# Delta-rule stage: key and query products on each head's own 64 rows instead of zero-padded keys, and output products that alternate between two heads

## The chip, the core and the metric

The kernel runs on one core of a Trainium2 chip. The metric is the device time of one execution in microseconds. It is a whole decoder of four layers in one launch; the change touches the first of its fifteen stages, the attention of layer 0, which fills roughly the first 3.9 ms.

## What is computed

The stage computes a gated delta rule for a batch of B = 16 sequences of T = 128 tokens and D = 256 channels, with 8 heads of 64 channels and M = 8 modes a head. Each mode rotates keys and queries by its own angles and has its own decay and step size:

```python
H, DK, DV, M = (8, 64, 64, 8)
q = (x @ Wq).reshape(B, T, H, DK)     # k, v alike
beta = sigmoid((x @ Wbeta).reshape(B, T, H, M))
tg = sigmoid((x @ Wtg).reshape(B, T, H, M))
qr = _l2norm(_rotary(q, cos, sin)) * scale
kr = _l2norm(_rotary(k, cos, sin))
g = log(clip(tg * rho, 1e-06))
def step(S, inp):                      # one token, for all modes, sequences and heads
    S = S * exp(b_g)
    kv = einsum('mbhk,mbhkv->mbhv', k_t, S)
    dv = (v_t - kv) * b_beta
    S = S + k_t[..., :, None] * dv[..., None, :]
    o_t = einsum('mbhk,mbhkv->mbhv', q_t, S)
o = einsum('tmbhv,hm->bthv', ys, softmax(mode_logits)) * sigmoid(x @ Wg)
x = layernorm(x + o @ Wo)
```

## The kernel before

The 16 sequences are 16 turns of one loop, each engine running its own instruction stream and meeting the others at semaphores. A turn does not step through tokens. For each of the 64 chains (8 heads x 8 modes) it forms two 128 x 128 matrices, key against key and key against query, multiplies them by the decays between tokens, inverts the lower triangular system in 32 x 32 blocks, and multiplies the solution by the key-query matrix. All of it is float32; one float32 `nc.tensor.matmul` shows in the trace as two MATMUL records, each with an LDWEIGHTS record.

A turn has two halves (`hf`) of 4 heads each. A half has 8 groups `i` of 4 chains, and 4 packs `p` of two groups. A pair of heads shares one 128-row tile: head 0 of the pair has its 64 channels on rows 0 to 63, head 1 on rows 64 to 127. Group `i` holds 4 modes of one head.

**Products.** For each pack, VectorE multiplies the keys and queries of a pair of heads by cosines (L951) and sines (L954), 4 modes at a time, GpSimd adds the two (L689) into `kq`, and ScalarE copies the keys of each head into `kz` (L880): `kz` holds zeros in the rows of the other head, written once (L658). For each group GpSimd spreads the decays under a mask (L684), TensorE sums them up to exponents (L764, and L765 in bfloat16, banks 0 and 1), ScalarE takes the exponential into `Bt` (L884), and TensorE multiplies the padded keys by keys and queries: 4 matmuls of 128 x 128 weights and 256 columns (L773) into two banks. VectorE then makes the coupling matrix `Lt` from them (L971, 4 a group) and the output matrix in place in `Bt` (L979). The products of group `i` wait until L979 is through with group `i - 2`, which used the same banks.

**Inverse.** `invert` on VectorE: transposes of the diagonal blocks (L1004), then a serial chain of 60 small operations (L1013, L1014). The products of the second half are worked off between the links of the first half's inverse: VectorE runs L951, L954, L971 and L979 of half 1 there, in a list (`between`) written out by hand.

**Solution.** TensorE solves 4 block rows `q` of 32 tokens: L793 and L796 couple a row to those before it, L806 applies the inverse. Their tiles are 32 to 128 rows by 32 columns, with 64 moving columns. ScalarE (L895, L899) or VectorE (L1024) evacuate them. Ahead of each group of 16 records a small bfloat16 matmul, `carrier` (L714), takes the wait. When a head's last block row is solved, GpSimd weights it (L696, `weighted`).

**Output.** L818: for each head 8 matmuls (modes) of 128 x 64 weights and 128 columns accumulate in bank 2, for an even head in partitions 0 to 63, for an odd one in 64 to 127. VectorE gates the result (L1030), L823 projects it after the second half, L128 to L154 add and normalise it, and the next turn starts at L745. The order on TensorE in a turn is: L745 to L750, products of both halves, L720 and L725 for the next turn, solution of half 0, output of half 0, solution of half 1, output of half 1, L823.

## Time and profile before

| | us |
|---|---|
| median of 3 runs | 8310.44 |
| lowest and highest of them | 8294.9, 8350.9 |
| span of the profiled execution | 8333.2 |

The profiled execution is 23 us (0.3%) over the median, and inside the runs' own spread. Over the whole span TensorE is busy 81%, VectorE 48%, ScalarE 22%, GpSimd 17%. The delta-rule turns fill 97 to 3925 us; there TensorE is busy 3292 us, VectorE 2048 us, ScalarE 860 us and GpSimd 867 us of 3828, at a mean granted TensorE clock of 0.69 of full speed; in the rest of the kernel the clock is 0.81. The rows of one turn (from 1748 to 1990 us) are enough to read: the turns repeat, and the costs of one are to be multiplied by 16. In a timeline a row is a run of equal instructions: its start, the time from the first start to the last end, how many, and in brackets the idle time of the engine before it with what ended it. A matmul's end is modelled, so consecutive rows overlap by the last one's drain: the distance of starts is what counts.

### The profile page before, as it was taken

What the parts mean: (1) busy time and instruction counts of PE and PEld (TensorE: products, weight loads), DVE (VectorE), ACT (ScalarE), POOL (GpSimd) and SP (SyncE); (2) the same over time, 40 slices, a digit from 0 to 9 for tenths busy, and PEclk for the clock granted to TensorE, in tenths of its full rate; (3) what the DMA queues carried; (4) which work ended last, traced back from release to release, by engine and by line L of the source; (5) the groups of instructions that cost most, each with busy time, mean ns of one, the idle gap of its engine ahead of it and who ended that gap; (6) DMA issues with size and microseconds to landing.
All of it is one profiled execution on the core that took longest, in us unless ns stands there. A gap on an engine that the chain in (4) does not pass through costs nothing. (4 is left out here: it accounts for less than half of the span.)

```text
span 8333.2 us, 92849 instructions
## 1 busy us (share of the span) xinstructions
PE 6721.0 (81%) x34116; PEld 4705.7 (56%) x34116; DVE 3959.2 (48%) x8807; ACT 1842.1 (22%) x2726; POOL 1376.6 (17%) x1101
## 2 busy tenths in 40 slices
PE   5889888888888888898599998876476766778698
PEld 3666665666666566666456665554243543555454
DVE  7454455654445565444300003545487344554444
ACT  2222122222222222221121211222211233223111
POOL 2221122222212222221200001312000100222100
PEclk8776677676666767766799999877655777778899
DMA  0000000000000000000000000000000000000000
GB/s 26 1 1 1 1 1 1 1 1 1 1 1 1 1 1 1 1 1 14 35 11 21 21 11 6 0 25 13 2 1 8 20 4 4 3 17 6 4 17 23
DMA packets 13607, 64.63 MB, mean 8 GB/s; under 512 B 1168, under 2 KB 5648, under 8 KB 11152
## 3 DMA queue, kind: packets, MB, share of 16 engines
q1 hardware_dynamic: 13200, 59.09, 2.0%
q8 instruction: 270, 4.42, 0.2%
q14 instruction: 137, 1.12, 0.0%
HBM read 56.99 MB, written 2.10 MB: 7 GB/s over the span
## 5 line engine op out<-in xcount | busy, mean ns | idle before, releaser
L806 PE MATMUL psum<-arena,weights 32*32 32x64 f32 x8192 | 860.4, 287 | 0.0
L773 PE MATMUL psum<-arena 128*128 128x256 f32 x2048 | 596.8, 443 | 319.3 <-DVE arena L979 312.6
L806 PEld LDWEIGHTS psum<-arena,weights 32*32 32x32 f32 x8192 | 763.5, 152 | 5.8
L1219 PE MATMUL psum<-arena 128*128 128x512 f32 x1600 | 711.7, 599 | 59.5 <-DVE Y L1283 35.8
L773 PEld LDWEIGHTS psum<-arena 128*128 128x128 f32 x2048 | 448.3, 224 | 526.1 <-issue 349.5
L796 PEld LDWEIGHTS psum<-arena 32*32 32x32 f32 (+2 forms) x6144 | 591.0, 157 | 256.6 <-issue 253.9
L796 PE MATMUL psum<-arena 32*32 32x64 f32 (+2 forms) x6144 | 670.3, 293 | 0.0
L1231 PE MATMUL psum<-arena 128*128 128x256 f32 x2624 | 583.0, 380 | 4.1 <-DVE arena L1324 4.1
L1300 DVE SCALAR_TENSOR_TENSOR Y<-psum,arena,Y 128x256 f32<-128x256 f32 x416 | 172.5, 478 | 849.0 <-PE psum L1231 849.0
L1231 PEld LDWEIGHTS psum<-arena 128*128 128x128 f32 x2624 | 499.1, 190 | 111.7 <-issue 43.5
L144 POOL TENSOR_TENSOR arena<-arena,eps 128x4 f32<-128x4 f32 (+2 forms) x76 | 15.1, 199 | 3221.9 <-DVE arena L139 3221.9
L899 ACT COPY arena<-psum 32x512 f32<-32x512 f32 x512 | 295.6, 577 | 1120.9 <-PE psum L806 1120.9
L1219 PEld LDWEIGHTS psum<-arena 128*128 128x128 f32 x1600 | 306.1, 192 | 413.6 <-issue 344.8
L689 POOL TENSOR_TENSOR arena<-arena 128x512 f32<-128x512 f32 x256 | 397.2, 1561 | 393.6 <-DVE arena L954 393.6
L1030 DVE TENSOR_TENSOR arena<-psum,arena 128x256 f32<-128x256 f32 x32 | 13.6, 425 | 938.7 <-PE psum L818 938.7
L696 POOL TENSOR_TENSOR arena<-arena 128x512 f32<-128x512 f32 x128 | 133.4, 1042 | 1782.2 <-ACT arena L899 1780.9
L1024 DVE TENSOR_TENSOR arena<-arena,psum 32x512 f32<-32x512 f32 x192 | 131.7, 686 | 566.5 <-PE psum L796 566.5
L422 PE MATMUL psum<-ident,arena 128*128 128x128 f32 x1280 | 217.6, 325 | 210.3 <-ACT arena L493 210.3
L402 PE MATMUL psum<-arena 128*128 128x512 f32 x640 | 357.6, 692 | 16.8 <-ACT arena L482 11.2
L1013 DVE TENSOR_TENSOR arena<-weights,arena 128x30 f32<-128x30 f32 (+14 forms) x960 | 359.2, 374 | 22.1
L1014 DVE TENSOR_TENSOR arena<-arena 128x30 f32<-128x30 f32 (+14 forms) x960 | 351.1, 366 | 20.8
L414 PEld LDWEIGHTS psum<-arena 128*128 128x128 f32 x2048 | 284.7, 217 | 101.6 <-issue 61.5
(418 smaller groups left out, 10541.0 us busy)
## 6 DMA issues: line engine op xcount, KB each, us to landing
arena<-in_experts_L_ffn SPq DMA_DIRECT2D x8, 2052.0 KB, 8.2
arena<-in_ctxT SPq DMA_DIRECT2D x16, 512.0 KB, 3.5
arena<-in_experts_L_ffn SPq DMA_DIRECT2D x18, 384.0 KB, 3.0
weights<-in_w_L_ffn SPq DMA_DIRECT2D x1, 3072.0 KB, 9.8
weights<-in_w_L_attn SPq DMA_DIRECT2D x1, 3024.5 KB, 13.1
weights<-in_w_L_ffn SPq DMA_DIRECT2D x1, 2753.0 KB, 12.8
weights<-in_w_L_relu SPq DMA_DIRECT2D x1, 2436.0 KB, 9.4
X<-in_x SPq DMA_DIRECT2D x1, 2048.0 KB, 8.3
```

Source lines behind the costliest of these rows:

```text
L402: mm = nc.tensor.matmul(out[:, b * 4:b * 4 + 4, :], qT[:, c, u * P:(u + 1) * P], km[:, at % 2, b * 4:b * 4 + 4, :], start=True, stop=True)
L414: mm = nc.tensor.matmul(o_psum[:, c * HH + h, :], pT[:, j % 2, h, :], v, start=True, stop=True)
L422: mm = nc.tensor.transpose(pt_psum[:, h, :], pr[:, j % 2, h, :], k.ident[:, :])
L689: pool.tensor_tensor(both, both, t1[:, j, :, :], ALU.add).then_inc(s["rotated"], 1)
L773: mm = nc.tensor.matmul(ps[:, 2 + 2 * hh + m // 2, (m % 2) * 2 * P:(m % 2 + 1) * 2 * P], kz[:, p % 2, hh, m, :], kq[:, p % 2, m, :, :], st ...
L796: mm = nc.tensor.matmul(ps[rows, 4 + h, m * DK:(m + 1) * DK], Lt[0:q * Q, h * M + m, rows], ur[0:q * Q, h, m, :], start=(hf == 1), stop=(h ...
L806: mm = nc.tensor.matmul(ps[rows, 4 + h, m * DK:(m + 1) * DK], Tt[rows, h * M + m, :], rhs, start=True, stop=True)
L899: nc.scalar.copy(ur[rows, h, :, :], ps[rows, 4 + h, :].rearrange("p (m e) -> p m e", e=DK)).then_inc(s["solution_ready"], 1)
L1013: linked(dve.tensor_tensor(part, bc(lanes[:, j + 1:, j], 2, j), bc(inv[:, j, 0:j], 1, below), ALU.mult))
L1014: linked(dve.tensor_tensor(inv[:, j + 1:, 0:j], inv[:, j + 1:, 0:j], part, ALU.add))
L1219: mm = nc.tensor.matmul(ps[:, bank, :], W[s][name][:, c, f * P:(f + 1) * P], xT[:, g, c, :], start=(c == 0), stop=(c == C - 1))
L1231: mm = nc.tensor.matmul(out, h[:, m % 2, f, u * P:(u + 1) * P], W[s]["w2"][:, f, :], start=(f == 0), stop=(f == FC - 1))
```

## The change

Keys are no longer copied. The key and query products of a head read `kq` on that head's own 64 rows, as weights and as moving data. A group `i` now holds 2 modes of each head of the pair instead of 4 modes of one head, and its 4 matmuls alternate between the heads, so between rows 0 to 63 and rows 64 to 127; head 0 writes one bank and head 1 the other. The helper `four` addresses such a group in `Bt` (two runs of two matrices) where `chains` took four in a row. GpSimd's masked decays (L684) become two instructions of half the size for each group, since the decays of a group no longer stand in a row. `kz`, its memset, ScalarE's copies (two for each pack), the semaphore `keys_padded` and TensorE's wait on it go. In the output products the two heads of a pair alternate, mode by mode, so partitions 0 to 63 and 64 to 127 of the bank alternate; TensorE waits for both weighted heads of a pair before it starts the pair, two waits in a half instead of four. The number of matmuls, their columns and the number of VectorE instructions stay.

```diff
...
-    def chains(i):
-
-        at = (i // 4 * 2 + i % 2) * M + i // 2 % 2 * 4
-        return slice(at, at + 4)
+    def four(ap, i):
+
+        heads, modes = slice(i // 4 * 2, i // 4 * 2 + 2), slice(i % 4 * 2, i % 4 * 2 + 2)
+        return ap.rearrange("p (h m) t -> p h m t", m=M)[:, heads, modes, :]
 
     def flat(ap):
         letters = "abcd"[:len(ap.shape) - 1]
@@ -620,7 +620,6 @@
     v, gateT, bt = A(W), A(PAIRS, P), A(2 * DHEADS * M)
     qkT, qkS = A(2, PAIRS, P), A(2, PAIRS, P)
     kq = A(2, 4, 2, P)
-    kz = A(2, 2, 4, P)
     t1, gm = A(2, 4, P), A(2, 4, P)
     qkn, squares = flat(t1), flat(gm)
     Ls, Bs = [A(CH, P) for _ in range(HALVES)], [A(CH, P) for _ in range(HALVES)]
@@ -654,8 +653,7 @@
         def _(pool):
             k.wait_weights(pool, stage)
             pool.memset(exponent, -0.5)
-            pool.memset(tiny, 1e-6)
-            pool.memset(flat(kz), 0.0).then_inc(s["consts_ready"], 1)
+            pool.memset(tiny, 1e-6).then_inc(s["consts_ready"], 1)
             pool.wait_ge(s["consts_ready"], 1)
 
             def stage_x(g):
@@ -680,9 +678,11 @@
                             i = 2 * p + hh
                             if hf or i >= 2:
                                 pool.wait_ge(s["exponents_ready"], u * GROUPS + i - 1)
-                            at = (hf * HALF + p // 2 * 2 + hh) * M + p % 2 * 4
-                            pool.tensor_tensor(gm[:, hh, :, :], bc(decay[:, at:at + 4], 2, P), bc(w.incl, 1, 4),
-                                               ALU.mult).then_inc(s["masked_decays"], 1)
+                            for head in range(2):
+                                at = (hf * HALF + p // 2 * 2 + head) * M + i % 4 * 2
+                                a = pool.tensor_tensor(gm[:, hh, 2 * head:2 * head + 2, :], bc(decay[:, at:at + 2], 2, P),
+                                                       bc(w.incl, 1, 2), ALU.mult)
+                            a.then_inc(s["masked_decays"], 1)
                             for j in range(2 if hh == 0 else 0):
                                 pool.wait_ge(s["halves_ready"], n * 2 + j + 1)
                                 both = kq[:, p % 2, :, j, :]
@@ -766,12 +766,14 @@
                                          ).then_inc(s["exponents_ready"], 1)
                         if hh == 0:
                             pe.wait_ge(s["rotated"], (u * NPACKS + p + 1) * 2)
-                            pe.wait_ge(s["keys_padded"], u * NPACKS + p + 1)
                         if hf or i >= 2:
                             pe.wait_ge(s["outputs_ready"], n - 1)
-                        for m in range(4):
-                            mm = nc.tensor.matmul(ps[:, 2 + 2 * hh + m // 2, (m % 2) * 2 * P:(m % 2 + 1) * 2 * P],
-                                                  kz[:, p % 2, hh, m, :], kq[:, p % 2, m, :, :], start=True, stop=True)
+                        for m in range(2):
+                            for head in range(2):
+                                rows = slice(head * DK, (head + 1) * DK)
+                                mm = nc.tensor.matmul(ps[:, 2 + 2 * hh + head, m * 2 * P:(m + 1) * 2 * P],
+                                                      kq[rows, p % 2, 2 * hh + m, 0, :], kq[rows, p % 2, 2 * hh + m, :, :],
+                                                      start=True, stop=True)
                         mm.then_inc(s["products_ready"], 1)
 
                 pe.wait_ge(s["outputs_ready"], (g + 1) * HALVES * GROUPS)
@@ -812,11 +814,12 @@
                             swap(g + 1)
                     if hf:
                         pe.wait_ge(s["o_gated"], g * HALVES + 1)
-                    for h in range(HALF):
-                        pe.wait_ge(s["weighted"], u * HALF + h + 1)
+                    for pair in range(HALF // 2):
+                        pe.wait_ge(s["weighted"], u * HALF + 2 * pair + 2)
                         for m in range(M):
-                            mm = nc.tensor.matmul(ps[h % 2 * DK:(h % 2 + 1) * DK, 2, (hf * 2 + h // 2) * P:(hf * 2 + h // 2 + 1) * P],
-                                                  ur[:, h, m, :], Bt[:, h * M + m, :], start=(m == 0), stop=(m == M - 1))
+                            for h in (2 * pair, 2 * pair + 1):
+                                mm = nc.tensor.matmul(ps[h % 2 * DK:(h % 2 + 1) * DK, 2, (hf * 2 + pair) * P:(hf * 2 + pair + 1) * P],
+                                                      ur[:, h, m, :], Bt[:, h * M + m, :], start=(m == 0), stop=(m == M - 1))
                     mm.then_inc(s["o_ready"], 1)
                 pe.wait_ge(s["o_gated"], (g + 1) * HALVES)
                 for c in range(PAIRS):
@@ -874,15 +877,10 @@
                     u = g * HALVES + hf
                     for p in range(NPACKS):
                         n = u * NPACKS + p
-                        act.wait_ge(s["rotated"], n * 2 + 1)
-                        for hh in range(2):
-                            rows = slice(hh * DK, (hh + 1) * DK)
-                            a = nc.scalar.copy(kz[rows, p % 2, hh, :, :], kq[rows, p % 2, :, 0, :])
-                        a.then_inc(s["keys_padded"], 1)
                         for i in (2 * p, 2 * p + 1):
                             act.wait_ge(s["exponents_ready"], u * GROUPS + i + 1)
-                            nc.scalar.activation(Bs[hf][:, chains(i), :],
-                                                 ps[:, i % 2, :].rearrange("p (c t) -> p c t", t=P),
+                            nc.scalar.activation(four(Bs[hf], i),
+                                                 ps[:, i % 2, :].rearrange("p (h m t) -> p h m t", h=2, t=P),
                                                  ACT.Exp).then_inc(s["decay_ready"], 1)
                 if more:
                     squared(g + 1)
@@ -959,24 +957,24 @@
                 steps = []
                 for i in (2 * p, 2 * p + 1):
                     n = (g * HALVES + hf) * GROUPS + i
-                    c0 = chains(i).start
                     Lt, Bt = Ls[hf], Bs[hf]
-                    kk = ps[:, 2 + 2 * (i % 2):4 + 2 * (i % 2), :].rearrange("p b (c k t) -> p (b c) k t", c=2, k=2)
-
-                    def coupling(m, n=n, c0=c0, kk=kk):
+                    kk = ps[:, 2 + 2 * (i % 2):4 + 2 * (i % 2), :].rearrange("p h (m k t) -> p h m k t", m=2, k=2)
+
+                    def coupling(m, n=n, i=i, kk=kk):
                         if m == 0:
                             dve.wait_ge(s["products_ready"], n + 1)
                             dve.wait_ge(s["decay_ready"], n + 1)
-                        at = hf * CH + c0 + m
-                        a = dve.scalar_tensor_tensor(out=Lt[:, c0 + m, :], in0=kk[:, m, 0, :],
-                                                     scalar=minus_beta[:, at:at + 1], in1=Bt[:, c0 + m, :],
+                        c = (i // 4 * 2 + m // 2) * M + i % 4 * 2 + m % 2
+                        at = hf * CH + c
+                        a = dve.scalar_tensor_tensor(out=Lt[:, c, :], in0=kk[:, m // 2, m % 2, 0, :],
+                                                     scalar=minus_beta[:, at:at + 1], in1=Bt[:, c, :],
                                                      op0=ALU.mult, op1=ALU.mult)
                         if m == 3:
                             a.then_inc(s["blocks_ready"], 1)
 
                     def outputs(n=n, i=i, kk=kk):
                         dve.wait_ge(s["blocks_ready"], n + 1)
-                        dve.tensor_tensor(Bt[:, chains(i), :], kk[:, :, 1, :], Bt[:, chains(i), :], ALU.mult
+                        dve.tensor_tensor(four(Bt, i), kk[:, :, :, 1, :], four(Bt, i), ALU.mult
                                           ).then_inc(s["outputs_ready"], 1)
                     steps += [lambda m=m, f=coupling: f(m) for m in range(4)] + [outputs]
                 return steps
```

## Rows read from the trace of the kernel before

**Rows 1.** One turn's stretches: length, busy (count) of PE, PEld, DVE, ACT, POOL; PEclk.

```profile
1764.50:1799.90 35.40, 32.08 (x111) 21.29 (x112) 32.70 (x59) 13.86 (x22) 26.68 (x21) 0.92 0.00 0
...
1799.90:1851.20 51.30, 29.65 (x77) 17.81 (x75) 49.52 (x117) 8.45 (x15) 14.30 (x10) 0.77 0.00 1
...
1851.20:1923.10 71.90, 71.90 (x510) 48.98 (x510) 31.96 (x70) 17.94 (x31) 6.26 (x5) 0.58 0.00 1
...
1931.00:1982.50 51.50, 51.50 (x475) 46.87 (x474) 8.66 (x13) 8.66 (x15) 3.13 (x3) 0.53 0.00 1
```

**Rows 2.** Timeline of VectorE, one pack of the first half.

```profile
1782.44 0.68 DVE L951 TENSOR_TENSOR arena<-arena,weights 128x512 f32<-128x512 f32 x1
...
1784.24 1.76 DVE L954 TENSOR_TENSOR arena<-arena,Y 128x512 f32<-128x512 f32 x1
...
1785.92 1.11 DVE L971 SCALAR_TENSOR_TENSOR arena<-psum,arena 128x128 f32<-128x128 f32 x4
...
1789.44 0.68 DVE L951 TENSOR_TENSOR arena<-arena,weights 128x512 f32<-128x512 f32 x1
```

**Rows 3.** VectorE before L971: timeline, first pack; last line, all turns.

```profile
1770.61 1.13 DVE L971 SCALAR_TENSOR_TENSOR arena<-psum,arena 128x128 f32<-128x128 f32 x4 [0.24 <-PE psum L773]
...
1773.41 1.12 DVE L971 SCALAR_TENSOR_TENSOR arena<-psum,arena 128x128 f32<-128x128 f32 x4 [0.95 <-PE psum L773]
...
  PE psum L773: 36.8, 56
```

**Rows 4.** Timeline of TensorE, one group of the first half.

```profile
1782.71 1.02 PE L764 MATMUL psum<-arena,weights 128*128 128x512 f32 x2
...
1783.57 0.38 PE L765 MATMUL psum<-arena 128*128 128x512 bf16 x1
...
1783.79 1.89 PE L773 MATMUL psum<-arena 128*128 128x256 f32 x8
```

**Rows 5.** Timeline of GpSimd: smallest operation, two groups' decays, last weighting.

```profile
1751.39 0.19 POOL L144 TENSOR_TENSOR arena<-arena,eps 128x1 f32<-128x1 f32 x1 [9.41 <-DVE arena L139]
...
1780.30 2.04 POOL L684 TENSOR_TENSOR arena<-arena,weights 128x512 f32<-128x512 f32 x2
...
1740.94 1.04 POOL L696 TENSOR_TENSOR arena<-arena 128x512 f32<-128x512 f32 x1 [0.91 <-ACT arena L899]
```

**Rows 6.** Timeline of TensorE: solution groups with a carrier between their starts.

```profile
1697.26 1.91 PE L796 MATMUL psum<-arena 32*32 32x64 f32 x16
...
1699.21 1.91 PE L796 MATMUL psum<-arena 32*32 32x64 f32 x16
```

**Rows 7.** Timeline of TensorE: outputs of halves 1, 0 and again 1.

```profile
1740.18 7.32 PE L818 MATMUL psum<-arena 128*64 128x128 f32 x64
...
1923.09 7.99 PE L818 MATMUL psum<-arena 128*64 128x128 f32 x64
...
1982.48 7.33 PE L818 MATMUL psum<-arena 128*64 128x128 f32 x64
```

**Rows 8.** L818 alone, two stretches: length, busy (count) of PE, PEld; PEclk.

```profile
1923.10:1925.60 2.50, 2.50 (x12) 2.50 (x13) 0.50 0.00 0
...
1925.60:1926.50 0.90, 0.90 (x10) 0.90 (x9) 0.50 0.00 0
```

**Rows 9.** Granted clock of four stretches, columns as in group 1.

```profile
1920.30:1927.10 6.80, 6.80 (x50) 6.45 (x48) 0.00 (x0) 1.19 (x3) 3.17 (x4) 0.50 0.00 0
...
1927.10:1933.90 6.80, 6.80 (x94) 6.61 (x93) 0.42 (x1) 1.15 (x2) 0.00 (x0) 1.00 0.01 2
...
1742.90:1753.00 10.10, 6.59 (x61) 5.79 (x59) 1.98 (x6) 0.00 (x0) 1.10 (x3) 1.00 0.01 3
...
1770.20:1804.20 34.00, 27.37 (x104) 18.21 (x102) 32.51 (x60) 12.16 (x20) 24.25 (x20) 1.00 0.00 0
```

**Rows 10.** Timeline of TensorE: what follows the outputs of half 0 and half 1.

```profile
1931.12 4.48 PE L806 MATMUL psum<-arena,weights 32*32 32x64 f32 x64
...
1748.01 1.99 PE L823 MATMUL psum<-weights,arena 128*128 128x256 f32 x8 [0.52 <-DVE arena L1030]
```

More of the change, by code:

```diff
@@ L604, in delta_stage @@
     qk_turned qkT_ready swapped swapped_ready decays_clipped decays_ready consts_ready tables_ready
-    angles_ready reduced halves_ready rotated keys_padded masked_decays exponents_ready decay_ready products_ready
+    angles_ready reduced halves_ready rotated masked_decays exponents_ready decay_ready products_ready
     blocks_ready outputs_ready blocks_taken inverse_ready solved coupled solution_ready rest_ready weighted
```

## Prediction, made before the change was run

> **What bounds the kernel now.** I read the page first and it decides little: the change touches one stage, so its shares mix that stage with fourteen others. The table of one turn by stage carries the argument [rows 1]; one turn is 242.3 us, the distance between two outputs of half 1 [rows 7], and 16 turns follow each other. In the first half of the products (1764.5 to 1799.9) VectorE is busy 32.7 of 35.4 us, in the second half with the inverse worked in (1799.9 to 1851.2) 49.5 of 51.3. From 1851.2 on TensorE is busy without a gap: 71.9 of 71.9, then the outputs, then 51.5 of 51.5. So products are bound by VectorE, solutions and outputs by TensorE.
>
> In the first half a pack takes VectorE 7.0 us, start of L951 to start of the next pack's (1782.44 to 1789.44), with no idle in it [rows 2]. TensorE needs for a group 0.86 us (L764) + 0.22 (L765), both from the distances of starts, and for L773 1.89 less the 0.16 by which such rows overlap, so 1.7: 2.8 us a group, 5.6 of the pack's 7.0 [rows 4]. Products are late for VectorE only at a few places: 0.24 and 0.95 us in the first pack of a turn, and over the whole stage 36.8 us in 56 waits, 2.3 us a turn [rows 3]; what is left of the 2.3 lies at the end of the second half.
>
> **Clock.** Granted clock is one of two levels, 1.0 (2.4 GHz) or 0.50 (1.2 GHz). It is 1.00 from 1770.2 to 1804.2, with TensorE busy 27.4 of 34.0 us; 0.50 from 1920.3 to 1927.1, where half 0's outputs start; 1.00 in the 6.8 us after that, and 1.00 from 1742.9 to 1753.0, which begins inside half 1's outputs [rows 9]. The solutions run mostly at the lower level (0.58 and 0.53 on the mean) although TensorE never stops [rows 1]. So outputs do two things: their own work, and the clock rises in them.
>
> **Outputs alternate (L818).** Today the 8 matmuls of a head follow each other in one half of the columns. Half 0's take 7.9 us (1923.09 until the next row's start at 1931.0), half 1's 7.3 [rows 7]. How fast could two heads go? At one level, 0.50, there are 12 records in 2.5 us while one head runs alone, 0.21 us each, and 10 in 0.9 us where the end of one head and the start of the next run together, 0.09 each [rows 8]. That is the overlap the edit makes permanent: 64 records in 32 slots, of 0.21 us at the lower level and 0.105 at the upper. The Trainium skill, "TensorEngine Tiling (Array Packing)", Key Properties, says that different tiles run in parallel, with which this row agrees; the same list says that a change of tiling mode drains TensorE, and alternating two heads of one shape is no such change.
>
> Half 0, if the clock rises when it does now (1927.1): 4.0 us at the lower level are 19 slots, 13 more take 1.4 us, 5.4 in all, 2.5 saved. The stretch at the upper level then meets more of the 64 records of L806 that follow. They have 64 columns against 128, so half a slot: 64 x 0.053 = 3.4 us if all are inside, against 4.48 today [rows 10]. The outputs and these end at 1923.1 + 5.4 + 0.1 + 3.4 = 1932.0, not 1935.6: 3.6 us saved. Bounds: 2.5 (L806 gains nothing) and 5.4 (the 1.9 us of upper level left after 1932.0 halve the next solutions too, worth 1.8). I take 3.6.
>
> Half 1: 2.6 us at the lower level until 1742.8 are 12.4 slots, the other 19.6 take 2.1: 4.7 instead of 7.3, 2.6 saved. L1030, L823 and the normalisation are a serial chain behind it and move up whole. The joint wait costs nothing: a weighting takes 1.04 us, the last starts at 1740.94 and ends at 1742.0 [rows 5], and the second pair starts only when the first is through, 16 x 0.21 = 3.4 us after 1740.2. Cover gone (all at the upper level), 1.7 us after the start, the wait would be 0.1 us.
>
> **Products on 64 rows (L773).** Same number of records and columns, alternating between rows 0 to 63 and 64 to 127, in two banks. No row of before has two row tiles at work; the nearest is the output's two column tiles [rows 8]. If they overlap as those do, 1.7 us becomes 0.86, and 3.4 at the lower level 1.7. Against that stand two changes of shape for each group, between L765, L773 and the next L764. Bounded by the carrier: groups of 16 records of 64 columns start 1.95 us apart at the lower level [rows 6]; at half a slot of 0.21 each, 1.68 of it is matmuls, so 0.27 for a carrier and a change of shape on both sides of it. I take all 0.27, nothing being the lower bound. The skill's drain rule (same page and list) gives no figure; by 0.27 a drain is not what would decide here. Each group is shorter by 0.6 us at the upper level, by 1.4 at the lower, most of it hidden behind VectorE; what it can give back is VectorE's 2.3 us a turn [rows 3]. I take 2.1 (0.66 at one late wait is hardly covered), 0 to 2.3.
>
> **GpSimd's decays** (L684) cost 1.02 us a group, 2.04 for two [rows 5]. Two instructions of half the size add a start: between nothing and 0.19 us, the whole of the smallest operation. I take 0.15. The first is on the path at the start of a turn, since VectorE waits for GpSimd there: 0.15 a turn. The others are covered by idle GpSimd (26.7 busy of 35.4 [rows 1]), but L954 stretches from 0.69 to 1.1 us (two in 1.76) where GpSimd works [rows 2]; two groups' extra 0.3 us may hold VectorE 0.1 to 0.2 in each of some four packs: 0.6, between 0 and 1.2. Products in sum: 2.1 - 0.15 - 0.6 = 1.4 us a turn.
>
> **Nothing else pays.** ScalarE's copies of keys, the memset, L979's and L884's new order of addresses: same sizes, and ScalarE is busy 13.9 of 35.4 us and 8.5 of 51.3 [rows 1], so freeing it is worth nothing; were that cover gone, a copy would have cost 0.6 us a pack half.
>
> **Sum.** 3.6 + 2.6 + 1.4 = 7.6 us a turn, 16 turns: 122 us. The profiled 8333.2 would be 8211; it stands 23 over the median of 8310.4, so the median goes to 8188.
>
> **Rivals.**
> A, the clock keeps the gain. It was 1.00 under 80% busy; with half the product time TensorE is busy about 2.2 of 3.5 us a group. If it fell there, a group would take 1.7 + 0.43 + 1.7 + 0.27 = 4.1 us against VectorE's 3.5: 0.6 x 6 groups = 3.6 lost, products -2.2. If it also no longer rose in the shorter outputs: half 0 with L806 6.7 + 0.1 + 6.7 = 13.5 against 12.5, -1.0; half 1 6.7 against 7.3, +0.6, but L823, 1.99 us [rows 10], doubles, less its tail -1.6: -1.0. Together -4.2 a turn, 67 us more: 8377, slower. It decides only if both outputs stay low. For it: L773 goes from 80% to some 60% busy. Against: the rise came 2.6 us into half 1's outputs, which still last 4.7. The skill, "TensorE: Matmul & The Clock Gate", "What's actually happening", has the clock throttled by default and released by activity; by that rule alone this rival would be the forecast.
> B, the row tiles take turns. Then L773 keeps 1.7 and adds 0.27: 3.1 us a group, still under 3.5, but nothing of the 2.1 comes back and four waits lengthen, -1.1, and with GpSimd -1.9. 3.6 + 2.6 - 1.9 = 4.3, x 16 = 69: 8241.
> C, the column tiles overlap only at heads' borders, as now. Products alone, 1.4 x 16 = 22: 8288. Rows 8 speak against it.
> D, the upper level also lasts through more of what follows: 5.4 in half 0, 2.6 and half of L745's lower-level time, say 1.2, in half 1, 2.1 in the products: 11.3, x 16 = 181: 8129.
>
> **Chances.** Forecast 0.50, A 0.12, B 0.15, C 0.08, D 0.15. The range goes from D to C, 8125 to 8290, leaving out A and the tails. One per cent of the median, about what a measurement of this kernel can tell from no change, is 83 us: faster means under 8227. That is D, 0.42 of the forecast's 0.50 and 0.05 of B: 0.62. Slower (over 8393) is the worse part of A, 0.08. The rest, 0.30, is within 1%.
>
> **What would show it.** L818: 64 records in 4.7 to 5.4 us instead of 7.3 and 7.9. L773 after a wait: 8 records over about 0.9 us at the upper level; if over 1.7, B. VectorE's waits for L773 near nothing; L684 in twice the count at 0.5 to 0.6 us. Clock 1.00 in the second part of each output and over most of the first half; else A. The turn 242.3 to about 235 us. I am wrong if VectorE's pack grows beyond 7.0 us, or if the stretches at the upper level shrink by as much as the outputs do.

## The result and the profile after

The changed kernel takes 8069.89 us, median of 3 runs (8062.1 to 8074.12), against 8310.44: ratio 0.970, 95% interval 0.966 to 0.973, 3.0% faster. 241 us were gained where 122 were forecast; the time lies below the range. The profiled execution went from 8333.2 to 8060.3 us, by 273 us.

Stretches of one turn of the kernel after, columns as in [rows 1]. The outputs of half 1 start at 1421.91, VectorE's first pack at 1445.65, the transposes of the inverse at 1480.07, the solution of half 0 at 1529.3; the outputs of half 0 at 1591.97 and those of half 1 at 1647.26 close it. The first line begins with the first pack.

```profile
1445.20:1480.10 34.90, 26.48 (x110) 12.30 (x110) 32.11 (x60) 6.29 (x11) 27.71 (x31) 0.90 0.00 0
1480.10:1529.30 49.20, 27.11 (x72) 12.34 (x73) 48.47 (x117) 4.63 (x9) 15.25 (x15) 0.69 0.00 1
1529.30:1591.97 62.67, 62.63 (x510) 42.69 (x510) 32.01 (x70) 18.09 (x32) 6.26 (x5) 0.68 0.01 1
1591.97:1647.26 55.29, 55.29 (x538) 50.66 (x537) 8.66 (x13) 9.21 (x16) 4.17 (x4) 0.56 0.00 1
```

The turn is 225.3 us instead of 242.3, 17.0 less. The third line holds the largest part of it, 9.2 us, and the diff touches nothing there: the solution of half 0 takes 62.7 us instead of 71.9 with the same 510 matmuls and TensorE busy throughout in both. Only the granted clock differs, 0.68 against 0.58. In the last turn, where it is 0.58 in the one and 0.57 in the other, the same stretch takes 67.3 and 67.7 us.

Timeline of TensorE in the kernel after: outputs of half 1 and what follows them, a first group of products and one after a wait, outputs of half 0 and what follows.

```profile
1421.91 5.45 PE L821 MATMUL psum<-arena 128*64 128x128 f32 x64
1427.89 1.99 PE L826 MATMUL psum<-weights,arena 128*128 128x256 f32 x8 [0.53 <-DVE arena L1028]
...
1446.89 2.08 PE L774 MATMUL psum<-arena 64*128 64x256 f32 x8 [1.10 <-POOL arena L689]
1448.93 2.07 PE L764 MATMUL psum<-arena,weights 128*128 128x512 f32 x2
...
1467.96 1.13 PE L774 MATMUL psum<-arena 64*128 64x256 f32 x8 [2.52 <-DVE arena L977]
1469.02 1.12 PE L764 MATMUL psum<-arena,weights 128*128 128x512 f32 x2
...
1591.97 5.75 PE L821 MATMUL psum<-arena 128*64 128x128 f32 x64
1597.65 0.18 PE L714 MATMUL psum<-arena 128*128 128x1 bf16 x1
1597.75 3.76 PE L808 MATMUL psum<-arena,weights 32*32 32x64 f32 x64
1601.44 0.18 PE L714 MATMUL psum<-arena 128*128 128x1 bf16 x1
...
1602.56 0.18 PE L714 MATMUL psum<-arena 128*128 128x1 bf16 x1
```

Outputs take 5.4 and 5.7 us instead of 7.3 and 8.0 [rows 7]; eight products 1.07 us from their start to the next row's, instead of 1.7 [rows 4].

VectorE in the kernel after: the one wait of a turn for products and the pack's length (timeline), then the waits of all turns (total, times, longest).

```profile
1453.24 1.12 DVE L969 SCALAR_TENSOR_TENSOR arena<-psum,arena 128x128 f32<-128x128 f32 x4 [2.06 <-PE psum L774]
...
1462.44 0.74 DVE L949 TENSOR_TENSOR arena<-arena,weights 128x512 f32<-128x512 f32 x1
...
1469.49 0.74 DVE L949 TENSOR_TENSOR arena<-arena,weights 128x512 f32<-128x512 f32 x1
...
DVE arena L969 <- PE psum L774: 30.7, 16, 2.2
```

**Where the 273 us went.** For every kernel I split each turn at three starts of rows of the timeline: "products" runs from the start of half 1's outputs to the first carrier of half 0's solution, "solution 0" to the start of half 0's outputs, "solution 1" (with those outputs) to the next outputs of half 1. Means over turns 2 to 16, in us, and the time per turn at the upper clock level inside solution 0. Labels are those of the experiments below; the last turn, which has no next chunk's keys to transpose, and one irregular turn of e12 are in the means.

```
                          products  solution 0  solution 1   turn   upper level in solution 0
before                      110.9      70.1        59.0      240.0      12.8
e1 outputs only             108.8      66.4        55.0      230.1      17.5
e2 products only            108.8      59.7        57.6      226.2      26.9
after                       107.1      60.5        55.3      222.9      26.2
e3 before, more transposes  111.2      63.9        59.0      234.1      22.4
e4 after, 16 carriers       106.7      60.4        55.3      222.4      27.1
e7 after, more transposes   106.5      60.3        54.9      221.7      28.3
e8 head by head             107.1      59.6        55.3      221.9      28.0
e9 before with fillers      108.8      59.3        36.6      204.7      33.6
e10 after with fillers      105.0      52.3        34.4      191.7      42.1
e12 before, clock held      108.8      50.8        36.6      196.2      45.6
e11 after, clock held       104.3      50.2        34.4      188.9      46.4
```

The means hide that there are only a few kinds of turn. Of turns 2 to 15, the kernel before has twelve with a solution 0 of 70.2 to 71.9 us and two of 61.6; e1 has seven of 71.9 and seven of 59.9 to 61.6; the kernel after nine of 62.6 and five of 55.4. An edit moves the mean by how many turns of each kind there are.

Before to after: 3.9 in products, 9.6 in solution 0, 3.7 in solution 1. What the sum of the prediction covered, products and solution 1, is 7.6 us a turn, as its 7.6. That the two agree to the tenth is partly luck: half 0 gave more than its term, half 1 less, and the products gave theirs in another place (see why the prediction was wrong, below). The miss is the middle column. The experiments had to show whether that column is the clock alone, and which edit moves it.

### The profile page after: what moved, and what is told of

It reads as the page before. It is cut to its first block and busy times, and to the rows that moved or that the text cites. A ratio compares the mean times of both kernels' runs of the same rounds, so it can differ in the third digit from the quotient of the medians.

```text
span 8060.3 us, 92655 instructions
## 1 busy us (share of the span) xinstructions
PE 6332.2 (79%) x34059; PEld 4271.2 (53%) x34116; DVE 3934.2 (49%) x8807; ACT 1680.9 (21%) x2470; POOL 1422.8 (18%) x1356
## 5 line engine op out<-in xcount | busy, mean ns | idle before, releaser
L808 PE MATMUL psum<-arena,weights 32*32 32x64 f32 x8192 | 781.7, 270 | 0.0
L774 PE MATMUL psum<-arena 64*128 64x256 f32 x2048 | 379.0, 499 | 428.4 <-DVE arena L977 405.9
L808 PEld LDWEIGHTS psum<-arena,weights 32*32 32x32 f32 x8192 | 690.8, 141 | 5.8
L798 PE MATMUL psum<-arena 32*32 32x64 f32 (+2 forms) x6144 | 600.4, 272 | 0.0
L1229 PE MATMUL psum<-arena 128*128 128x256 f32 x2624 | 583.1, 380 | 4.1 <-DVE arena L1322 4.1
L774 PEld LDWEIGHTS psum<-arena 64*128 64x128 f32 x2048 | 234.3, 238 | 632.0 <-issue 435.9
L1229 PEld LDWEIGHTS psum<-arena 128*128 128x128 f32 x2624 | 499.1, 190 | 111.7 <-issue 43.5
L1217 PEld LDWEIGHTS psum<-arena 128*128 128x128 f32 x1600 | 306.1, 192 | 413.5 <-issue 344.7
L764 PE MATMUL psum<-arena,weights 128*128 128x512 f32 x512 | 344.0, 759 | 57.1 <-POOL arena L683 57.1
L683 POOL TENSOR_TENSOR arena<-arena,weights 128x256 f32<-128x256 f32 x512 | 338.6, 688 | 176.7 <-ACT arena L875 169.2
L882 ACT ACTIVATE arena<-psum 128x512 f32<-128x512 f32 x256 | 152.9, 597 | 1006.5 <-PE psum L765 672.4
```

What stands on the lines that cost most here:

```text
L683: a = pool.tensor_tensor(gm[:, hh, 2 * head:2 * head + 2, :], bc(decay[:, at:at + 2], 2, P), bc(w.incl, 1, 2), ALU.mult)
L764: nc.tensor.matmul(bank, w.after, gm[:, hh, :, :], start=True, stop=False)
L774: mm = nc.tensor.matmul(ps[:, 2 + 2 * hh + head, m * 2 * P:(m + 1) * 2 * P], kq[rows, p % 2, 2 * hh + m, 0, :], kq[rows, p % 2, 2 * hh + m ...
L798: mm = nc.tensor.matmul(ps[rows, 4 + h, m * DK:(m + 1) * DK], Lt[0:q * Q, h * M + m, rows], ur[0:q * Q, h, m, :], start=(hf == 1), stop=(h ...
L808: mm = nc.tensor.matmul(ps[rows, 4 + h, m * DK:(m + 1) * DK], Tt[rows, h * M + m, :], rhs, start=True, stop=True)
L1217: mm = nc.tensor.matmul(ps[:, bank, :], W[s][name][:, c, f * P:(f + 1) * P], xT[:, g, c, :], start=(c == 0), stop=(c == C - 1))
```

## Experiments

**One edit at a time (e1, e2).** e1 is the kernel before with the alternating outputs only:

```diff
-                    for h in range(HALF):
-                        pe.wait_ge(s["weighted"], u * HALF + h + 1)
+                    for pair in range(HALF // 2):
+                        pe.wait_ge(s["weighted"], u * HALF + 2 * pair + 2)
                         for m in range(M):
+                            for h in (2 * pair, 2 * pair + 1):
...
```

e2 is the kernel after with this loop put back as it was.

> The kernel before with the output products alone alternating between two heads; padded keys, their copies and the whole decays stay. Two theories of the 17.0 us a turn that the change gave back in the profiled executions (242.3 to 225.3). Theory 1 (clock): the solution of half 0, which the diff does not touch, went from 71.9 to 62.6 us a turn because the granted clock was at the upper level for 22.5 us of it and not 11.1; that is a matter of where its instructions fall, and belongs to neither edit. Then this kernel shows outputs of about 5.5 us instead of 7.3 and 7.9, and the path from outputs of half 0 to those of half 1 shorter by about 4 us: 6 us a turn, 95 us, 8215; if the clock also rises in the solution of half 0 as it does in the changed kernel, 9 to 16 us a turn more, and the solution's length and its time at the upper level move together. Rival (work): the edits themselves gave all of it and add up; then this kernel and the one with the products alone share the 250 us, and the solution of half 0 is shorter in the one whose edit shortens it, at the same time at the upper level.

> The changed kernel with the output products in the old order, head by head: the products on 64 rows, the split decays and the missing key copies alone. Theory 1 (clock): from the end of the outputs to the first solution 2 us a turn less (waits of VectorE for products 36.8 us in all before, 2.3 a turn, now partly back), 30 us, 8280, unless the clock changes in the solution of half 0, which would show in the time at the upper level and is worth 9 us a turn for each 10 us of it. Rival (work): together with the kernel that has the outputs alone it makes up 250 us at unchanged time at the upper level.

Measured: e1 8153.67 us, ratio 0.978 (0.975 to 0.981); e2 8126.39, 0.975 (0.972 to 0.979), beside 8335.93 for the kernel before. Singly they gain 182 and 210 us, 392 together and so more than the 241 to 273 of both: the gains don't add. By the table e1 takes 2.1 us a turn off products (half 1's outputs stand in that stretch) and 4.0 off solution 1, e2 2.1 off products, near what was costed. The 1.3 us that e2 takes off solution 1, where it changes nothing, are clock again: nine of its turns 2 to 15 have 10.2 us or more at the upper level there, of the kernel before two; the rest have 6.8. But either edit alone also brings more of the upper level into solution 0, most of all the products (59.7 us against 70.1), which end well ahead of it.

**What precedes the rise (e3, e4, e7).** In the kernel after the clock rises at 1562.04, 2.3 us behind the end of the transposes of the next chunk's keys and queries (L732). Timeline of TensorE in the kernel after around them:

```profile
1557.74 1.97 PE L732 MATMUL psum<-ident,arena 128*128 128x128 f32 x8
...
1559.64 1.91 PE L795 MATMUL psum<-arena,ident 128*32 128x512 f32 x2
```

Stretches of the kernel after around the rise, columns as in [rows 1]:

```profile
1529.34:1562.04 32.70, 32.70 (x226) 22.52 (x227) 30.53 (x70) 8.23 (x15) 3.13 (x2) 0.53 0.01 1
1562.04:1572.28 10.24, 10.24 (x121) 7.08 (x119) 1.44 (x1) 3.46 (x6) 0.00 (x0) 1.00 0.01 2
1572.28:1579.11 6.83, 6.83 (x27) 3.45 (x25) 0.00 (x0) 2.32 (x4) 0.00 (x0) 0.50 0.00 0
1579.11:1589.35 10.24, 10.24 (x121) 7.36 (x119) 0.00 (x0) 3.46 (x6) 1.04 (x1) 1.00 0.01 2
```

The same transposes in the timeline of the kernel before, and two stretches of it:

```profile
1880.65 1.97 PE L732 MATMUL psum<-ident,arena 128*128 128x128 f32 x8
```

```profile
1851.20:1910.06 58.86, 58.86 (x368) 39.16 (x369) 31.96 (x70) 13.89 (x24) 3.13 (x2) 0.51 0.00 1
1910.06:1920.30 10.24, 10.24 (x120) 7.37 (x119) 0.00 (x0) 3.44 (x6) 1.00 (x1) 1.00 0.01 2
```

In this turn of the kernel before, eight records of transposes (four transposes) in 1.8 us are followed by no rise, and the clock stays at the lower level to 1910.06; after, the same eight are followed by two stretches at the upper level. But it isn't a matter of the kernel. One of the two short turns of the kernel before, its transposes and three stretches of it:

```profile
449.48 1.97 PE L732 MATMUL psum<-ident,arena 128*128 128x128 f32 x8
```

```profile
422.13:483.73 61.60, 61.60 (x509) 42.37 (x509) 32.00 (x70) 17.93 (x31) 6.27 (x5) 0.69 0.01 1
425.26:452.57 27.31, 27.31 (x169) 17.80 (x166) 25.39 (x62) 6.82 (x12) 3.15 (x2) 0.50 0.01 1
452.57:462.81 10.24, 10.24 (x114) 6.73 (x114) 3.49 (x8) 3.14 (x6) 0.00 (x0) 1.00 0.01 2
```

Here the rise comes behind the same eight records too, in the same code. e3 makes the block larger in the kernel before (the two transposes of keys are issued twice more ahead of the four real ones, which overwrite them; eight records more), e7 does so in the kernel after:

```diff
                 pe.wait_ge(s["qk_normalised"], g + 1)
+                for _ in range(2):
+                    for c in range(PAIRS):
+                        nc.tensor.transpose(ps[:, 0, c * P:(c + 1) * P], qkn[:, c * P:(c + 1) * P], k.ident)
                 for j in range(2):
```

e4 puts `for _ in range(16): carrier()` at that place of the kernel after, one-column matmuls that were to shift the block by 1.7 us.

> The kernel before with work added: the four transposes of the keys' half of L732 (128 x 128, full array) are issued twice more ahead of the real ones, 16 more records in each turn but the last, in the middle of the solution of half 0. Their result is overwritten. Theory 1 (clock): the dense work lifts the clock there, as it rose in the changed kernel after the same place (1562.0, with the transposes from 1557.7 to 1559.5): time at the upper level in the solution of half 0 from 11 to over 20 us, and the turn is 5 to 9 us shorter in spite of 1.7 to 3.5 us more work: 8180 to 8240. Rival (work): nothing changes but the work: 1.7 to 3.5 us a turn longer, 8340 to 8365.

> The changed kernel with 16 more carriers (bfloat16, one column) ahead of L732, which move the transposes and all behind them later by about 1.7 us and add next to nothing to the array's load. Rival (work): 1.7 us a turn, 25 us longer, 8095. Theory 1 (clock): what counts is where the transposes fall; either the rise of the clock after them is kept and the turn is 0 to 2 us longer, or it is lost and the turn is 8 to 11 us longer (8200 to 8250). A result that is not near 8095, with the time at the upper level in the solution of half 0 changed by the same amount, tells for theory 1.

> The changed kernel with the transposes of L732 for the keys issued twice more, as in the kernel before with the same addition. In the changed kernel most turns have the solution of half 0 at the upper level for 22.5 us of 62.6 and a third of them for 36.1 of 55.4. Theory 1 (clock): the addition costs 1.7 to 3.5 us a turn and can win only where a turn still lacks a stretch at the upper level: 8000 to 8100, and the length of the solution follows its time at the upper level at 0.7 to 0.8 us for each us, less the added work. Rival (work): 8100 to 8125.

Measured: e3 8240.02 us, ratio 0.989 (0.985 to 0.992): more work, and 1.1% faster. e4 8053.02, 0.966 (0.962 to 0.969); e7 8046.79, 0.967 (0.965 to 0.969), both at the kernel after or just under it. (The 16 carriers of e4 shifted the block by only 0.5 us, from 28.3 to 28.85 us behind the start of the solution, so e4 says little.) A typical turn of e3, columns as before:

```profile
411.53:476.82 65.29, 65.29 (x517) 45.37 (x517) 31.96 (x70) 17.91 (x31) 6.27 (x5) 0.66 0.00 1
412.46:446.60 34.14, 34.14 (x219) 23.97 (x217) 31.04 (x70) 8.08 (x14) 3.14 (x2) 0.50 0.01 1
446.60:456.84 10.24, 10.24 (x122) 7.09 (x121) 0.00 (x0) 3.46 (x6) 0.00 (x0) 1.00 0.01 2
```

With eight more records the solution takes 65.3 us in nine turns and 60.4 to 60.7 in five, not 71.9: the clock rises within 3 us of the larger block's end in all of turns 2 to 15. So the old order of products and outputs, with not one instruction of either changed, gives a shorter solution 0 too. Over the eight kernels above without fillers the column falls with the last one, from 70.1 at 12.8 to about 60 at 28, some 0.67 us for each us at the upper level.

**Do row tiles need the alternation (e8).** The products' loop of the kernel after with the heads outermost, so that four matmuls on rows 0 to 63 precede four on rows 64 to 127:

```diff
-                        for m in range(2):
-                            for head in range(2):
+                        for head in range(2):
+                            for m in range(2):
```

> The changed kernel with the 4 matmuls of a group of products in the order head 0, head 0, head 1, head 1 and not alternating. It tells whether the two blocks of 64 rows run beside each other only when they alternate. If so the 8 records take about 1.9 us at the upper level, or 1.4 to 1.5 with the overlap at the border of the heads, and not 1.13. VectorE hides most of it: 0 to 1.5 us a turn longer, 8070 to 8095, unless the clock in the solution of half 0 moves.

Measured: 8053.54 us, ratio 0.968 (0.966 to 0.970), as the kernel after. Timeline of its TensorE, a group after a wait:

```profile
1458.51 1.14 PE L774 MATMUL psum<-arena 64*128 64x256 f32 x8 [2.30 <-DVE arena L977]
1459.58 1.53 PE L764 MATMUL psum<-arena,weights 128*128 128x512 f32 x2
```

1.07 us again: for eight records of products it is the head's own 64 rows that count, and not the order. (A matmul in f32 is two records, so a head has four of them.) For the output products the order counts: 16 records of one head in a row overlapped at the border only [rows 8].

**Can the clock be bought outright (e5, e6, e9, e10).** In the solutions TensorE works on tiles of 32 to 128 rows by 32 columns. Fillers are small matmuls on the diagonal tiles that the solution leaves unused at the moment, into the carrier's bank, whose content nobody reads. e5 has them in f32 on the kernel after, e6 in bf16; e10 is the same kernel as e6, and e9 puts the same fillers into the kernel before:

```diff
+            def filler(r):
+                at = slice(r * Q, (r + 1) * Q)
+                nc.tensor.matmul(ps[at, 3, :], ident_h[at, at], later_h[at, :, :], start=True, stop=True)
...
                                 for m in range(M):
+                                    if q == 1 and m % 4 < NQ - 1:
+                                        filler(1 + m % 4)
...
                             for m in range(M):
+                                if m % 4 < NQ - 1:
+                                    filler((q + 1 + m % 4) % NQ)
```

> The changed kernel with work added to hold the clock: in each solution group of L808, and of L798 in the second block row, three float32 matmuls of 32 x 32 weights and 512 columns on the other three blocks of rows, into bank 3, which nothing reads then. Theory 1 (clock): the solutions, now at the lower level for most of their 118 us a turn although TensorE never stops, go to the upper level; if the fillers run beside the real work, as the alternating heads do, a group of 16 records takes about 1.1 us and not 1.95 and the turn gets up to 40 us shorter: 7500 to 7800. Rival: small tiles do not run beside each other unless they alternate record by record; then each group is longer by up to 2.5 us and the kernel is slower than 8070, up to 9500.

> As the kernel with float32 fillers, but with bfloat16 matmuls of 512 columns (one record each), six in a group spread between the real ones. Theory 1 (clock) with tiles that run beside each other: 7500 to 7800. Rival (they take turns): six times 0.21 to 0.43 us more a group, 8500 or more.

> The kernel before with the bfloat16 fillers that took the changed kernel to 7549 in one look. With the clock held at the upper level in the solutions of both kernels, the difference between them is what the edits themselves take off, free of where the clock happens to rise. By the terms of my sum: outputs in 64 slots of 0.11 us against 32, 7.0 against 3.6 in each half, so 3.4 x 2 = 6.8 us a turn; products 2 us a turn; 8.8 x 16 = 140 us: this kernel at about 7690. Rival (the gain of the change lies in work that I have not seen, in the solution of half 0): the difference is 250 us as without fillers, 7800. If the fillers help only beside the changed products, this kernel stays above 8000.

> The changed kernel with the bfloat16 fillers again, timed in rounds beside the kernel before and beside the kernel before with the same fillers. Theory 1 (clock): 7550, as in the one look, and 140 us under the kernel before with fillers. Rival: 250 us under it.

Measured: e5 7669.93 us and e6 7548.94, one run each; e10 7556.57, ratio 0.908 (0.906 to 0.911); e9 7771.91, 0.933 (0.930 to 0.936). Timeline of TensorE in e10, two groups of the solution with their carriers and the first of their fillers, then the outputs of half 0:

```profile
1525.44 0.18 PE L714 MATMUL psum<-arena 128*128 128x1 bf16 x1
1525.55 0.38 PE L719 MATMUL psum<-arena 32*32 32x512 bf16 x1
...
1526.56 0.18 PE L714 MATMUL psum<-arena 128*128 128x1 bf16 x1
1526.66 0.39 PE L719 MATMUL psum<-arena 32*32 32x512 bf16 x1
...
1564.50 3.83 PE L830 MATMUL psum<-arena 128*64 128x128 f32 x64
```

A group takes 1.12 us with its six fillers, against 1.95 without and at the lower level [rows 6]. Here, 64 outputs all at the upper level take 3.76 us to the next row's start; in e9, one head at a time, 5.99. Yet e9 and e10 were 215 us apart, where theory 1 had 140 and the rival 250: 7.0 us a turn of their difference of 13.0 lay again in solution 0. The clock wasn't held there. In both, TensorE stands idle for 4.3 us inside that stretch, waiting for VectorE ahead of the transposes (from 1529.98 in e10), and the clock falls: for 6.83 us in e10 (1532.32 to 1539.15), for 30.7 in a typical turn of e9 (1637.06 to 1667.79). That difference was the last thing open.

**Both kernels with the clock held (e11, e12).** e11 is e10, e12 is e9, each with a dense block ahead of the wait at which TensorE stood those 4.3 us:

```diff
+                for _ in range(18):
+                    nc.tensor.matmul(ps[:, 3, :], ident_h, later_h[:, :, :], start=True, stop=True)
                 pe.wait_ge(s["qk_normalised"], g + 1)
```

> The kernel after with the fillers, and 18 dense matmuls (128x128 by 128x512, bf16, into bank 3, never read) issued by TensorE ahead of its wait for the normalised keys of the next chunk, where it stands 4.28 us per turn. Theory (the granted clock in the solution of half 0 is the part of the gain that the sum lacked): with no idle left there the granted clock stays at the upper level through the whole solution of half 0, which then takes about 46.5 us in place of 51.2; over 15 turns some 70 us, so about 7490 us. Rival (something in the changed order itself slows or speeds this stretch, and the clock only accompanies it): the stretch stays at 51 us and the time at 7555 us; 18 x 0.21 us of matmul also lengthen it if the wait was shorter than they are.

> The kernel before with the same fillers and the same 18 dense matmuls. Theory: the solution of half 0 takes the same 46.5 us per turn as in the changed kernel with the clock held, so that the two differ by the edits' own work alone: outputs 2.24 us in each half and 1.5 us of products per turn, 6.0 us x 16 = 96 us, and this kernel takes about 7586 us. Rival (the change speeds the solution itself, beyond the clock): the two keep the 215 us between them that the pair with fillers alone showed, and the solution of half 0 stays some 7 us longer here than in the changed kernel.

Measured, beside 8317.0 us for the kernel before: e11 7516.74 us, ratio 0.903 (0.901 to 0.905), the fastest of all; e12 7623.87, 0.916 (0.913 to 0.919). Windows of e11 (products, solution 0, solution 1), then of e12:

```profile
1390.14:1494.49 104.35, 69.36 (x284) 34.47 (x282) 86.28 (x190) 17.28 (x27) 47.82 (x53) 0.77 0.00 1
1494.49:1543.46 48.97, 48.68 (x647) 33.18 (x647) 32.09 (x70) 17.83 (x31) 5.57 (x5) 1.00 0.01 2
1543.46:1577.87 34.41, 34.41 (x659) 31.46 (x658) 8.66 (x13) 9.23 (x16) 4.18 (x5) 1.00 0.01 2
```

```profile
1455.43:1564.36 108.93, 74.83 (x284) 49.65 (x282) 87.68 (x190) 27.13 (x43) 44.86 (x37) 0.86 0.00 1
1564.38:1613.34 48.96, 48.68 (x648) 33.16 (x648) 32.05 (x70) 17.80 (x31) 5.58 (x5) 1.00 0.01 2
1613.34:1649.98 36.64, 36.64 (x660) 33.83 (x658) 8.66 (x13) 9.21 (x16) 4.17 (x5) 1.00 0.01 2
```

At the upper level throughout, solution 0 takes 48.97 us in the one and 48.96 in the other. The theory had 46.5 from a mere subtraction of the idle, and so both times come out above those expected (7490 and 7586). The equality it asked for is there to 0.01 us, and the rival's 7 us are gone. The two medians are 107 us apart, 6.7 us a turn, where 96 were expected; the four runs of e12 lie 44 us apart, so this is good to about 1.5 us a turn (an estimate). The turns shown give 4.6 us in products and 2.2 in solution 1. This is what the edits are worth with the clock up in both solutions. In the products it isn't held (0.77 and 0.86), so what a lower clock costs the changed kernel there is in it. Without fillers the change gains 17.2 us a turn, and 9.6 of them are clock in solution 0.

## Why the prediction was wrong, step by step

**The sum's own terms held in total, but not one by one.** Half 0: the outputs took 5.68 us to the next row's start (forecast 5.4), the 64 records of L808 3.7 (3.4), the clock rose 4.2 us after the start (4.0). From the start of the outputs to the end of these 64 it is 9.5 us instead of 12.4, 3.0 of the forecast 3.6; the clock stays up to 1603.00, past their end, and that gives another 1.1 in the next groups, as the upper bound had allowed. Half 1: from the start of the outputs to L826 5.98 us instead of 7.83 (L823, [rows 10]), 1.85 saved and not 2.6. The step that was off is the moment of the rise: 2.6 us into the outputs before, 3.6 us after. At one level the slot was right; L821 alone, both stretches of half 1's outputs (columns PE, PEld, clock):

```profile
1421.91:1425.51 3.60, 3.60 (x34) 3.60 (x36) 0.50 0.02 5
1425.51:1427.50 1.99, 1.85 (x34) 1.60 (x30) 1.00 0.00 0
```

34 records in 3.60 us are 0.21 us for a pair of heads, the 0.21 that rows 8 were read for.

**Products.** Eight records 1.07 us at the upper level (0.86 plus a part of the 0.27 was forecast) and 2.04 at the lower (1.7 plus the same). But the gain of 1.4 us doesn't come where the prediction put it. From VectorE's first pack to the transposes it is 34.42 us instead of 34.18 (1445.65 to 1480.07; 1765.74 to 1799.92), 0.2 more. The waits for products fell only from 36.8 to 30.7 us: 56 small ones became 16 of about 2 us, one a turn. There the clock falls at 1445.99, under the first group of products (2.08 us) and L764 behind it (2.07), as the rows above show. This is rival A's mechanism in small, 2 us once a turn and not at every group. Before, the clock is low there too, but only up to 1770.12, under the first group, and VectorE waits 0.24 and 0.95 us [rows 3]; after, it is low up to 1452.81, under the second group as well. In the second half the mean clock fell from 0.77 [rows 1] to 0.69, and four of the eight groups of half 1 take 2.08 us, but VectorE waits for none of them. A pack takes 7.05 us instead of 7.0, so GpSimd's halved instructions cost it 0.05 at most, not 0.1 to 0.2. (The prediction read the 1.76 us of [rows 2] as two instructions of L954; the row is one.) What came instead lies in the second half, 49.27 us instead of 51.28. VectorE there, all its instructions of two lines of the kernel before and the same two lines after (busy us, mean ns):

```profile
L1013 DVE TENSOR_TENSOR arena<-weights,arena 128x30 f32<-128x30 f32 (+14 forms) x30 | 12.5, 418 | 0.3
...
L971 DVE SCALAR_TENSOR_TENSOR arena<-psum,arena 128x128 f32<-128x128 f32 x32 | 11.1, 345 | 1.1 <-PE psum L773 1.1
```

```profile
L1011 DVE TENSOR_TENSOR arena<-weights,arena 128x30 f32<-128x30 f32 (+14 forms) x30 | 11.5, 384 | 0.3
...
L969 DVE SCALAR_TENSOR_TENSOR arena<-psum,arena 128x128 f32<-128x128 f32 x32 | 10.8, 338 | 0.0
```

1.1 us of idle for products gone, and by the stretches 1.0 us of VectorE's busy time (49.52 [rows 1] to 48.47). Over all turns the first of the two lines means 374 ns in the kernel before, in e1 and e3, and 357 to 360 in the kernel after, e2 and e8, so it goes with the edit of the products. That the line runs shorter because GpSimd's instructions are half as long fits, but it is not shown: no run here changed that alone.

**The step that failed** is one of omission. The prediction priced the clock only where the edits are: in the outputs, in the products, and right behind them. Of the solutions it said that they "run mostly at the lower level (0.58 and 0.53 on the mean) although TensorE never stops", and took that for fixed. It had the rows that said otherwise: 0.58 on the mean is not 0.50; there is a stretch of 10.24 us at the upper level in it (1910.06, shown above), and it ends at 1920.3, where [rows 9] begin. A stretch that comes and goes in an unchanged place can come earlier or twice. Priced by its ends, at the 0.8 us for each us that the two typical turns show (71.9 to 62.7 for 11.1 to 22.5), from the lower level throughout (8 us a turn lost) to two more such stretches (16 gained), it would have been the largest uncertainty of the sum and would have widened the range on both sides. Instead the low end, 8125, rested on rival D, which let the upper level last longer in the outputs and products alone; D's direction was right, its place wasn't, and its 59 us beyond the forecast are half of the 118 that were measured beyond it.

What the runs showed in its place: 9.6 us a turn of the 17.2 gained are in solution 0, at 26.2 us of upper level instead of 12.8, and with the clock up throughout solution 0 takes the same 48.97 us in both kernels (e11, e12).

Rivals B and C fell: row tiles overlap (1.07 us) and column tiles do throughout. A was right that the clock falls more in the products (61.1 us of upper level a turn in that stretch instead of 72.0), but VectorE waits for that at one place of a turn only, and the outputs kept their rise.

**The spread of before** may have been a hint as well. Its three runs lie 56 us apart. Two turns of 230 us stand among those of 242 in its trace, and these have a solution 0 of 61.6 us with the clock up for 23.7. Some five turns more or less of that kind would make that spread; it is not shown, since one run alone is traced. In the kernel after, 5 of 16 have a solution of 55.4.

The Trainium skill, "TensorE: Matmul & The Clock Gate", Loop structure matters more than you think, says that matmuls issued back to back keep the engine at its fast clock. The trace doesn't bear that out for this kernel: in solutions without a gap the granted clock is 0.58 and 0.53 [rows 1], and the fillers, which close no gap, bring it to 1.00 (solution 1 of e10 throughout, 34.41 us; solution 0 in e11, with the dense block).

**What stays open.** Why the same transposes are followed by a rise in some turns and not in others was not found. The traces narrow it down to when, not what. In the twelve long turns of the kernel before the eight records start 27.8 to 29.5 us behind the start of solution 0, and in the two short ones at 27.3; in the kernel after they start at 28.3 or, where the solution begins with 15.7 us at the upper level, at 20.9, and there the rise always comes. The level last fell 0.8 or 0.9 us behind the start of the solution in eleven of the long turns and 2.7 behind it in one, 3.1 in the two short ones, 2.1 or 15.7 in the kernel after. That fits a matter of where the same work falls between the changes of the clock, which both edits move, but what sorts the turns was not tested. And the cost of the two changes of shape was not measured alone; a group of eight products is 0.2 us above twice-overlapped records, which bounds it.

## What to carry to other kernels

Before an edit is priced, list the stretches in which the granted clock is neither wholly up nor wholly down and price each at both levels, also those that the diff doesn't touch; here that was over half of the gain. Where TensorE is busy with small tiles at the lower level, matmuls on idle tiles into a bank that nobody reads can be worth more than a better order of the real work: 8.4% here with the fillers and the dense block, 3.0% with the change, 9.7% together. To know what an edit is worth as work, compare both kernels with the clock held.

## What the hardware did that was not expected

- TensorE without a gap stays at the lower level for 51.1 us (1934.0 to 1985.1 in the kernel before, granted clock 0.50), nearly all of it on tiles 32 columns wide, and with eight more records of 128x128 transposes the block was followed by at least 10.24 us at the upper level in all of turns 2 to 15 (e3).
- Six bf16 fillers of 512 columns beside 16 matmuls of 64 columns on other tiles take nothing from them: 1.12 us from carrier to carrier at the upper level (e10), and 1.12 without fillers at that level in the kernel after (1601.44 to 1602.56).
- Tiles overlap without alternation as long as the other tile's work is only four records off (e8).
- More work made the kernel before 1.1% faster (e3).
